# A graph layer and a mixture of experts on one Trainium2 core: events tested at every slot, another cut of the groups, row additions moved from GpSimd to VectorE

## The chip, the cores and the metric

The kernel runs on one core of one Trainium2 chip, in one launch. The metric is the device time of a run in microseconds (us), lower is better. Slots, tiles and groups are counted in the order in which the kernel works, which is from the last node to the first.

## The reference

With x of 12,500 nodes x 256 in float32, and 200,000 edges (source, destination, weight) sorted by destination:

```python
support = layernorm(x) @ W
x = x + segment_sum(support[src] * weight[:, None], dst) + b
z = layernorm(x)                      # no scale, no shift
h = gelu(einsum('nd,edf->enf', z, W1) + b1)      # 8 experts, 256 -> 512
y = einsum('enf,efd->end', h, W2) + b2           # 512 -> 256
out = x + layernorm(w_dense-weighted sum of y + z) * gamma + beta
```

The two experts and their weights are chosen once, from the mean of z over all nodes, so they are the same for every node, and are known only when the last node's z is. The destinations are dense for low node numbers (a square law), and thin for high ones.

## The kernel before

The 12,500 nodes are 98 tiles of 128. They are taken in reverse: tile 0 holds the last nodes and gets about 8 slots of edges, the last tile 158. A slot is 128 edges; there are 1563 and a remainder.

**The edge loop** (85 to 1977 us). GpSimd (POOL) gathers the 128 source rows of a slot by an indirect DMA (L588) into a ring G of 64 slots and 8 more; it waits by `s_main` (the count of finished slots) with s - RING + 3. VectorE (DVE) makes the slot's one-hot matrix OH, weighted (L1087), in a ring of eight. TensorE (PE) adds OH times G to the tile's sums (`edge`, L1451; a float32 matmul is two records, so 3126 in all). PE's program runs 8 slots per turn of a hardware loop (`slots`). Behind every odd slot it calls `event`: a While over a register test (L1460), is the next event due here. A turn ends with the loop's own code (L1486, L1491). The events are planned by `events()` and come from a table EVT:

- END, at a tile's end, 97 times: `chores` (from L1396: the transposes of the last tile's sums, their product with W, the transpose of a finished row block) and then `begin` (L1411 to L1414). As the test is at odd slots alone, a tile's end falls within a pair of slots, and `begin` retakes both of the pair with one-hot matrices OHX of the next tile, which ScalarE (ACT) made in `match` (L656, L658) and `copy` (L668). EXTRA, 7 times, is `chores` alone.
- UPS, BOTH, DOWNS, 65 in all, for 64 units. A unit is one expert's work on one group of tiles ahead of the choice: `unit_up` (L1423, z times W1) and `unit_down` (L1434, h times W2). The first 8 groups are done ahead with all 8 experts; when the experts are known, VectorE picks the two. Group 0 has two tiles, so its 8 units are half units; `by_size` (L1437 to L1442) branches on that.

`events()` spreads the units over the tiles by `room`, an estimate of what time a tile's slots leave to PE, counted from tile 14 on.

ScalarE works in sections, one per tile's end: the copy of OHX and of the tile's sums AS (L670), AT (L675), the normalized block XH (L722, needs `root`'s NR and R), then X1, the transposed block YT, a square sum, the next tile's `match`; and at the end of a section in which a group's last tile came, `root` (L702 to L716, with a table load at L704), the deviations of the group's tiles.

**The choice** of experts lies from 1977 to about 1988 us.

**The groups behind it** (1988 to 2384 us): 17 groups of four tiles (68 tiles, `post`) go through the two chosen experts, with float32 values split in a high and a low part. Per group PE runs 8 steps (L1555 to L1565 up, L1586 down). ScalarE makes Ht and Hhi (L908, L911), VectorE Hlo (L1220) and the rest: `bias` on XN (L1226), `total` (L1245 to L1259: sum, mean and variance), `give` (L1266, L1271: scale by gamma, then times the deviation plus XL). VectorE's work for a group follows two loops behind, and that for the 8 groups done ahead is put beside it, one in every second loop. POOL's `add_rows` adds the bias to XN for the groups done ahead (L605, eight times) and beta to XL for all 25 (L607); POOL's `rstd` makes the power -0.5 (L612). The last two groups go by `finish` (L1287 to L1310) in the four pieces of PARTS, with a deviation from ScalarE and VectorE. SP stores the output (L551) and loads XL (L495).

PE's side of a tile's end, as the change finds it:

```python
for r in range(n):
    if r % 4 == 0:
        e.wait_ge(s_oh, a + (r + 4))
    edge(g, r)
    if r % 2 == 1:
        event(a, r, g)
```

Of the kernel before, what the change touches and what calls it, by code (L numbers as in the profile page):

```python
# [4 lines left out]
P = 128  # L5
# [16 lines left out]
GT = 4  # L22
XG = (NT + GT - 1) // GT
SMALL = 2
NG = (NT - SMALL + GT - 1) // GT + 1
AHEAD = 8
UNITS = AHEAD * E
# [15 lines left out]
def group(t):  # L43
    return 0 if t < SMALL else (t - SMALL) // GT + 1


def tiles(g):
    a = SMALL + (g - 1) * GT
    return range(a, min(a + GT, NT)) if g else range(SMALL)


def part(t):
    return slice((t - SMALL) % GT, (t - SMALL) % GT + 1)


def place_in(t):
    return t - tiles(group(t))[0]
# [11 lines left out]
def sections():  # L69
# [14 lines left out]
def events():  # L84
# [3 lines left out]
    room = [max(0.0, 0.75 * slots[t] - 3.5) * most[t] if t >= 14 else 0.0 for t in range(NT)]  # L88
    size = [len(tiles(k // E)) / GT for k in range(UNITS)] + [1.0]
    free, u, out = 0.0, 0, []  # L90
    for t in range(NT):
        free += room[t] * sum(size) / sum(room)
        n = 0
        while u + n <= UNITS and (free >= size[u + n] / 2 or t == NT - 1):
            free -= size[u + n]
            n += 1
# [17 lines left out]
def gnn_ffn(nc, x, dflat, srct, dstt, wt, W, b, Wr, br, W1, b1t, W2, b2, gamma, beta, cst, iota_e, evt, out):  # L114
# [13 lines left out]
    with ctx:  # L128
# [26 lines left out]
        XND = sb("XND", [P, 2])  # L155
# [34 lines left out]
        OHX, OHT = early("OHX", [P, 2, P]), early("OHT", [P, 2, 2, P])  # L190
# [106 lines left out]
        s_xn, s_xb, s_xc, s_xp = sem("act_xn"), sem("pool_xn"), sem("dve_xn"), sem("pool_x1")  # L297
# [83 lines left out]
        def _(e):  # L381
# [79 lines left out]
            for t, _, kind, n in EVENTS:  # L461
# [11 lines left out]
                if kind in (END, EXTRA):  # L473
                    keep_rows(n)
                    if n == tiles(post[0])[0] + 4 * GT:
                        for t in tiles(post[0]):
                            e.wait_ge(yt_st[t % 4], 16 * (t // 4 + 1))
                        e.dma_start(YL0[:, :, :], yt_d[post[0], :, :, :]).then_inc(yl_in[0], 16)
# [12 lines left out]
            e.dma_start(YL[:, 1, :, :], yt_d[post[1], :, :, :]).then_inc(yl_in[1], 16)  # L491
# [42 lines left out]
            for n, g in enumerate(order):  # L534
# [11 lines left out]
                elif n == NG - 1:  # L546
                    for _, some in PARTS[1:]:
# [13 lines left out]
        def _(e):  # L561
# [37 lines left out]
            def add_rows(n):  # L599
                g = order[n]  # L600
                m = len(tiles(g))
                e.wait_ge(s_xn, n + 1)
                if g < AHEAD:
                    e.wait_ge(s_b2, 2)
                    e.tensor_tensor(out=XN[:, n % 3, 0:m, :], in0=XN[:, n % 3, 0:m, :], in1=B2[:, :].unsqueeze(1).to_broadcast([P, m, D]), op=ALU.add).then_inc(s_xb, 1)  # L605
                e.wait_ge(gb_in, 32)
                e.tensor_tensor(out=XL[:, n % 4, 0:m, :], in0=XL[:, n % 4, 0:m, :], in1=be_bc[:, :].unsqueeze(1).to_broadcast([P, m, D]), op=ALU.add).then_inc(s_xp, 1)  # L607

# [5 lines left out]
            added = 0  # L614
            for n in range(NG):
                until = min(n + (2 if n + 1 < NG and order[n + 1] < AHEAD else 1), NG - 1)
                while added <= until:
                    add_rows(added)
                    added += 1
                if n < NG - 2:  # L620
                    rstd(n)

        @block.scalar
        def _(e):
# [25 lines left out]
            def match(t):  # L650
                e.load([row_r], THR[0:1, t - 1:t])
                odd = e.snap(row_r, min_val=1, max_val=NE - 1)
                step(e.activation(XND[:, :], ND[:, bass.ds(odd - 1, 2)], ACT.Identity, bias=t128_row[:, t:t + 1]))
                e.wait_ge(s_act, chain)
                for k in range(2):
                    step(e.activation(OHT[:, 0, k, :], iota, ACT.Abs, bias=XND[:, k:k + 1]))  # L656
# [1000 lines left out]
```

## Time and profile before

| | us |
|---|---|
| median of 3 runs | 2390.43 |
| lowest, highest | 2388.29, 2390.5 |
| span of the profiled execution | 2384.3 |
| PE busy in the span | 2211.0 (93%) |
| PE weight loads | 1730.4 (73%) |
| VectorE | 1052.3 (44%) |
| ScalarE | 1193.0 (50%) |
| POOL | 1598.6 (67%) |

The span is counted from the first instruction to the last of one profiled execution; no whole-run time stands beside it, and the runs' median is 6.1 us longer. Engine names in the rows: PE is TensorE's matmuls, PEld its weight loads, PEldq the instructions of its sequencer (registers, branches, semaphores), DVE VectorE, ACT ScalarE, POOL GpSimd, SPq the DMA issues of SyncE. In a row by source the three durations are the least, the median and the largest in ns, and behind them stand the first and the last start in us. "[4.13 <-X]" is the engine's idle time before the row and what ended it; "issue" is a wait that the profile puts down to nothing but the instruction not having been issued. The edge loop takes four fifths of the span. Matmul records overlap: their distance is shorter than their duration.

### The profile page before, as it was taken

How to read it: one execution, taken by the hardware profiler on the slowest of the kernel's cores; microseconds unless marked ns; L12 is line 12 of the kernel's file. 1: busy time of each engine (PE TensorE's matmuls, PEld its weight loads, DVE VectorE, ACT ScalarE, POOL GpSimd, SP SyncE). 2: the span in 40 equal slices, each digit the busy share in tenths (PEclk: the TensorE clock that was granted, in tenths of full speed). 3: DMA queues.
4: the chain of work that ended last, by engine and by line, in shares of the span. 5: the costliest groups of instructions: out<-in, count | busy, mean ns of one | idle time of the engine just before them, and what ended most of it. 6: DMA issues, size and time to landing. Idle time of an engine off the chain costs nothing. (4 is left out here: it accounts for less than half of the span.)

```text
span 2384.3 us, 41652 instructions
## 1 busy us (share of the span) xinstructions
PE 2211.0 (93%) x9949; PEld 1730.4 (73%) x9950; DVE 1052.3 (44%) x2924; ACT 1193.0 (50%) x3203; POOL 1598.6 (67%) x1626
## 2 busy tenths in 40 slices
PE   2488999899999999999999999999998999999998
PEld 1366777676776777777777777777776777999997
DVE  7883223232232223232322323232222235899999
ACT  3577667665665555545534343322324116656654
POOL 6777777777777777777777777777777772242341
PEclk9999999999999999999999999999999999999999
DMA  9955667665656665566656655656565554333422
GB/s 371 333 170 156 203 203 241 186 188 180 184 183 182 179 176 175 178 185 192 186 176 189 189 172 188 182 169 190 179 193 165 183 162 135 101 113 110 134 92 68
DMA packets 226740, 425.79 MB, mean 179 GB/s; under 512 B 36675, under 2 KB 134774, under 8 KB 226600
## 3 DMA queue, kind: packets, MB, share of 16 engines
q0 software_dynamic: 75008, 204.90, 28.6%
q1 hardware_dynamic: 151160, 217.12, 27.9%
q10 hardware_dynamic: 432, 2.40, 0.3%
q14 instruction: 113, 0.93, 0.1%
q8 instruction: 27, 0.44, 0.1%
HBM read 341.53 MB, written 82.75 MB: 178 GB/s over the span
## 5 line engine op out<-in xcount | busy, mean ns | idle before, releaser
L588 POOL DMA_INDIRECT G<-xr_d,SRC x1467 | 1391.7, 949 | 446.9 <-issue 302.5
L1087 DVE TENSOR_SCALAR OH<-CST,DL,WR 128x128 f32<-128x128 f32 x1563 | 569.2, 373 | 1271.0 <-PE ps L1451 1140.1
L1451 PE MATMUL ps<-G,OH 128*128 x3126 | 739.5, 389 | 78.7 <-DVE OH L1087 58.7
L1451 PEld LDWEIGHTS ps<-G,OH 128*128 128x128 f32 x3126 | 596.7, 194 | 224.8 <-issue 143.3
L1434 PE MATMUL ps<-W2u,H 128*128 128x256 f32 x1920 | 430.6, 382 | 6.8 <-issue 6.0
L1423 PE MATMUL ps<-YU,W1u 128*128 128x512 f32 (+1 forms) x1024 | 426.4, 569 | 9.7 <-ACT H L783 8.5
L1434 PEld LDWEIGHTS ps<-W2u,H 128*128 128x128 f32 x1920 | 362.7, 191 | 69.4 <-issue 20.8
L1423 PEld LDWEIGHTS ps<-YU,W1u 128*128 128x128 f32 x1024 | 195.1, 191 | 206.3 <-issue 184.9
L791 ACT ACTIVATE YE<-ps 128x512 f32<-128x512 f32 (+1 forms) x128 | 72.6, 569 | 442.2 <-PE ps L1434 442.1
L783 ACT ACTIVATE H<-ps,b1a 128x512 f32<-128x512 f32 (+1 forms) x256 | 168.6, 661 | 226.1 <-PE ps L1423 225.8
L612 POOL TENSOR_TENSOR ZR<-ZV,mhalf 128x4 f32<-128x4 f32 (+1 forms) x23 | 31.4, 1366 | 218.0 <-DVE ZV L1259 218.0
L668 ACT ACTIVATE OHX<-OHT,WR 128x128 f32<-128x128 f32 x194 | 67.4, 394 | 211.9 <-PE ps L1451 209.0
L908 ACT ACTIVATE Ht<-ps,b1s 128x512 f32<-128x512 f32 x136 | 93.8, 690 | 129.5 <-PE ps L1565 93.6
L1586 PE MATMUL ps<-W2h,Hlo 128*128 128x256 f32 x512 | 144.9, 283 | 0.0
L1586 PE MATMUL ps<-W2l,Hhi 128*128 128x256 f32 x512 | 144.8, 283 | 0.0
L1586 PE MATMUL ps<-W2h,Hhi 128*128 128x256 f32 x512 | 144.2, 282 | 0.0
L588 POOL DMA_INDIRECT G<-in_x,SRC x96 | 92.7, 965 | 42.7 <-issue 25.9
L1220 DVE TENSOR_TENSOR Hlo<-Ht,Hhi 128x512 fp32r<-128x512 f32 x136 | 108.2, 810 | 20.3 <-ACT Hhi L911 20.3
L1402 PE MATMUL ps<-Wsb,AT 128*128 128x256 f32 x416 | 108.0, 382 | 0.7 <-ACT ps L690 0.7
L1586 PEld LDWEIGHTS ps<-W2h,Hhi 128*128 128x128 f32 x512 | 97.8, 191 | 5.6
L1586 PEld LDWEIGHTS ps<-W2l,Hhi 128*128 128x128 f32 x512 | 97.8, 191 | 5.0
L1586 PEld LDWEIGHTS ps<-W2h,Hlo 128*128 128x128 f32 x512 | 97.8, 191 | 0.0
(221 smaller groups left out, 2395.8 us busy)
## 6 DMA issues: line engine op xcount, KB each, us to landing
W1u<-in_W SPq DMA_DIRECT2D x64, 512.0 KB
W2u<-in_W SPq DMA_DIRECT2D x64, 512.0 KB
y_d<-YE SPq DMA_DIRECT2D x56, 512.0 KB, 5.4
G<-xr_d,SRC POOLq DMA_INDIRECT x1467
x_d<-X SPq DMA_DIRECT2D x98, 128.0 KB
yt_d<-YT SPq DMA_DIRECT2D x98, 128.0 KB, 3.3
XR<-in_x SPq DMA_DIRECT2D x97, 128.0 KB, 3.2
XL<-x_d SPq DMA_DIRECT2D x24, 512.0 KB, 4.7
```

What stands on the lines that cost most here:

```text
L588: e.indirect_dma_start(out=G[0:rows(s), held(s), :], out_offset=None, in_=x if s < FRESH else xr_d, in_offset=bass.IndirectOffsetOnAxis(ap ...
L668: e.activation(OHX[:, k, :], OHT[:, 1, k, :], ACT.Copy, scale=WR[:, bass.ds(odd + k, 1)]).then_inc(s_ohx, 1)
L783: e.activation(H[:, i, 0:w], ps[:, UP[i % 2], 0:w], ACT.Gelu, bias=b1a[:, u % E, i:i + 1]).then_inc(s_gelu, 1)
L791: e.activation(YE[:, u % 2, p * w:(p + 1) * w], ps[:, DN[p], 0:w], ACT.Copy).then_inc(s_ye, 1)
L908: e.activation(Ht[:, i % HB, 0:w], ps[:, 4 + i % HB, 0:w], ACT.Gelu, bias=b1s[:, i // 4, i % 4:i % 4 + 1]).then_inc(s_ht, 1)
L1087: e.tensor_scalar(OH[:, s % OHR, :], iota, DL[:, s:s + 1], WR[:, s + 1:s + 2], ALU.is_equal, ALU.mult).then_inc(s_oh, 1)
L1220: e.tensor_tensor(out=Hlo[:, h, 0:w], in0=Ht[:, i % HB, 0:w], in1=Hhi[:, h, 0:w].bitcast(f32), op=ALU.subtract).then_inc(s_hlo, 1)
L1402: e.matmul(ps[:, XB, 0:D], AT[:, c * P:(c + 1) * P], Wsb[:, c, :], start=False, stop=True, skip_group_check=True)
L1423: ins = e.matmul(ps[:, UP[i % 2], 0:m * P], W1u[:, c, i * P:(i + 1) * P], YU[:, c, 0:m * P], start=(c == 0), stop=(c == 1))
L1434: ins = e.matmul(ps[:, DN[p], h * D:(h + 1) * D], H[:, i, j * P:(j + 1) * P], W2u[:, i, :], start=(h == 0 and i == 0), stop=(i == 3), skip ...
L1451: e.matmul(ps[:, 0, 0:D], OH[:, r, :], Gf[:, bass.ds(g + r * D, D)], start=False, stop=True, skip_group_check=True).then_inc(s_main, 1)
L1586: ins = e.matmul(acc, hp[:, h, rows], wp[:, x_, f, :], start=(i == 0 and q % 2 == 0 and a == 0), stop=(i == HID - 1 and a == 2), skip_grou ...
```

## The change

- The event test stands behind every slot, and the tables give a tile's end to the slot; `begin` retakes one slot, OHX and OHT are half as large, `match` and `copy` make one matrix. POOL's wait is s - RING + 2.
- `root` is called one section later, behind AT and ahead of the normalized block.
- The groups are cut anew: nine of four, one of two, fifteen of four. So the 8 groups done ahead are all full (32 tiles in place of 30), `by_size` goes, 17 groups with 66 tiles are left for behind the choice, and the second of these is that of two tiles. `room` is 0.8 x slots - 3.0, from tile 15 on.
- POOL's `add_rows` goes. VectorE does it in `stored_bias` and `beta_rows`, placed in steps of its loops. POOL keeps `rstd`, now for the last group but one too, which goes by `total` and `give`; PARTS has three pieces, all of the last group.

```diff
-SMALL = 2
-NG = (NT - SMALL + GT - 1) // GT + 1
 AHEAD = 8
+SMALL = NT - AHEAD * GT - (NT - AHEAD * GT) // GT * GT
+SIZES = [GT] * (AHEAD + 1) + [SMALL] + [GT] * ((NT - AHEAD * GT) // GT - 1)
+STARTS = [sum(SIZES[:g]) for g in range(len(SIZES))]
+NG = len(SIZES)
...
-        root = together.get(x1)
+        root = together.get(copied[v - 3]) if v >= 3 else None
+        waiting += root or []
         xh = waiting.pop(0) if waiting else None
-        waiting += root or []
...
-    room = [max(0.0, 0.75 * slots[t] - 3.5) * most[t] if t >= 14 else 0.0 for t in range(NT)]
-    size = [len(tiles(k // E)) / GT for k in range(UNITS)] + [1.0]
+    room = [max(0.0, 0.8 * slots[t] - 3.0) * most[t] if t >= 15 else 0.0 for t in range(NT)]
     free, u, out = 0.0, 0, []
     for t in range(NT):
-        free += room[t] * sum(size) / sum(room)
+        free += room[t] * (UNITS + 1) / sum(room)
...
-        PARTS = ((NG - 2, slice(0, len(tiles(order[NG - 2])))), (NG - 1, slice(0, 2)), (NG - 1, slice(2, 3)), (NG - 1, slice(3, 4)))
+        PARTS = (slice(0, 2), slice(2, 3), slice(3, 4))
...
-                    e.wait_ge(s_main, s - RING + 3)
+                    e.wait_ge(s_main, s - RING + 2)
...
-            def add_rows(n):
...
-            added = 0
-            for n in range(NG):
-                until = min(n + (2 if n + 1 < NG and order[n + 1] < AHEAD else 1), NG - 1)
-                while added <= until:
-                    add_rows(added)
-                    added += 1
-                if n < NG - 2:
-                    rstd(n)
+            for n in range(NG - 1):
+                rstd(n)
...
-                for k in range(2):
-                    e.activation(OHX[:, k, :], OHT[:, 1, k, :], ACT.Copy, scale=WR[:, bass.ds(odd + k, 1)]).then_inc(s_ohx, 1)
+                e.activation(OHX[:, :], OHT[:, 1, :], ACT.Copy, scale=WR[:, bass.ds(cut + 1, 1)]).then_inc(s_ohx, 1)
...
+                if s["root"] is not None:
+                    root(s["root"])
                 if s["xh"] is not None:
                     normal(v, s["xh"])
...
-                if s["root"] is not None:
-                    root(s["root"])
...
+            def stored_bias(n):
+                m = len(tiles(order[n]))
+                e.wait_ge(s_xn, n + 1)
+                e.wait_ge(s_b2, 2)
+                e.tensor_tensor(out=XN[:, n % 3, 0:m, :], in0=XN[:, n % 3, 0:m, :], in1=B2[:, :].unsqueeze(1).to_broadcast([P, m, D]), op=ALU.add).then_inc(s_xb, 1)
+
+            def beta_rows(n):
+                m = len(tiles(order[n]))
+                e.wait_ge(gb_in, 32)
+                e.wait_ge(s_xn, n + 1)
+                e.tensor_tensor(out=XL[:, n % 4, 0:m, :], in0=XL[:, n % 4, 0:m, :], in1=be_bc[:, :].unsqueeze(1).to_broadcast([P, m, D]), op=ALU.add).then_inc(s_xp, 1)
...
+                    if k >= 2 and k % 2 == 0 and i == 2:
+                        beta_rows(n)
                     if two and i == 2:
+                        stored_bias(n + 1)
                         total(n + 1, None, slice(0, 2))
...
+                    if two and i == 6:
+                        beta_rows(n + 1)
+                    if k >= 2 and k % 2 == 0 and i == 7 and k < len(post) - 1:
+                        beta_rows(place[post[k - 1]])
...
+                    if i == 5 and k == len(post) - 1:
+                        beta_rows(NG - 2)
                     if i == 6 and k == len(post) - 1:
                         bias(k)
+                        beta_rows(NG - 1)
+            n = NG - 2
+            total(n, len(post) - 2, slice(0, 2))
+            total(n, len(post) - 2, slice(2, 4))
+            give(n, slice(0, 4))
             for j in range(len(PARTS)):
                 finish(j)
...
             def begin(v, g):
-                e.wait_ge(s_ohx, v * 2)
+                e.wait_ge(s_ohx, v)
                 e.wait_ge(s_as, v + 1)
-                e.matmul(ps[:, 0, 0:D], OHX[:, 0, :], Gf[:, bass.ds(g, D)], start=True, stop=False, skip_group_check=True)
-                e.matmul(ps[:, 0, 0:D], OHX[:, 1, :], Gf[:, bass.ds(g + D, D)], start=False, stop=True, skip_group_check=True).then_inc(s_begin, 1)
+                e.matmul(ps[:, 0, 0:D], OHX[:, :], Gf[:, bass.ds(g, D)], start=True, stop=True, skip_group_check=True).then_inc(s_begin, 1)
...
-            def by_size(do):
...
                         with e.If(now > UPS):
-                            by_size(unit_down)
+                            unit_down(e.snap(u_r, min_val=0, max_val=UNITS - 1))
...
                         with e.If(now == END):
-                            begin(e.snap(v_r, min_val=1, max_val=FINAL), g + (r - 1) * D)
+                            begin(e.snap(v_r, min_val=1, max_val=FINAL), g + r * D)
...
                     edge(g, r)
-                    if r % 2 == 1:
-                        event(a, r, g)
+                    event(a, r, g)
...
-        "iota_e": (np.arange(NE) // 2 * 2).astype(np.float32)[None], "evt": evt,
+        "iota_e": np.arange(NE, dtype=np.float32)[None], "evt": evt,
```

## Rows read from the trace of the kernel before

**Rows 1.** Windows: busy us (instructions) by engine, clock, DMA share, GB/s.
```profile
700.00:1100.00 400.00, 383.84 (x1575) 287.88 (x1574) 117.57 (x323) 211.09 (x624) 302.63 (x320) 0.99 0.60 180
...
2001.00:2362.00 361.00, 361.00 (x2305) 328.10 (x2306) 338.68 (x620) 224.65 (x390) 113.08 (x56) 1.00 0.31 105
```

**Rows 2.** By source, gathers (L588) and edge matmuls (L1451): ns, starts.
```profile
L588 POOL DMA_INDIRECT G<-xr_d,SRC x1467: 903/946/1013, 136.1 to 1973.5; - x184
...
L1451 PE MATMUL ps<-G,OH x3126: 379/379/791, 85.2 to 1976.8; 128*128 x195, 128*128 128x256 f32 x1
```

**Rows 3.** Waits: us in total, times, longest.
```profile
DVE OH L1087 <- PE ps L1451: 1140.1, 230, 19.3
...
PEld ps L1451 <- issue: 143.3, 216, 47.3
...
DVE OH L1087 <- DMA G<-xr_d,SRC: 44.9, 37, 14.0
...
PE ps L1413 <- ACT AS L670: 35.7, 12, 4.1
...
PE ps L1423 <- ACT H L783: 8.5, 5, 3.6
```

**Rows 4.** By source, 1656.1 to 1659.7 (last: 1656.75 to 1657.15), eight slots.
```profile
L1451 PE MATMUL ps<-G,OH x16: 379/379/478, 1656.3 to 1659.6; 128*128 x16
...
L1451 PEldq FUSED_REGOPS  x9: 46/46/51, 1656.2 to 1659.7; - x9
...
L1460 PEldq MOVE  x4: 37/37/37, 1656.5 to 1658.4; - x4
...
L1460 PEldq COMPARE_BRANCH  x4: 201/204/207, 1656.6 to 1658.5; - x4
...
L1451 PEldq FUSED_REGOPS  x2: 46/46/46, 1656.8 to 1657.0; - x2
```

**Rows 5.** By source, the tests (L1460), whole span.
```profile
L1460 PEldq MOVE  x950: 37/37/38, 85.4 to 1975.5; - x190
```

**Rows 6.** By source, L1451, 1206 to 1208.5, behind a unit.
```profile
L1451 PEldq FUSED_REGOPS  x6: 46/46/51, 1206.3 to 1207.8; - x6
...
L1451 PE MATMUL ps<-G,OH x2: 379/379/379, 1208.2 to 1208.4; 128*128 x2
```

**Rows 7.** By source, L1460 then L1396, 1651 to 1653, a tile's end.
```profile
L1460 PEldq MOVE  x1: 37/37/37, 1651.5 to 1651.5; - x1
...
L1396 PEldq EVENT_SEMAPHORE  x1: 51/51/51, 1652.3 to 1652.3; - x1
```

**Rows 8.** Timeline of PE: start, us, count; a full unit, then half units.
```profile
1194.33 7.17 PE L1434 MATMUL ps<-W2u,H 128*128 128x256 f32 x32 [0.31 <-issue]
...
1201.33 7.03 PE L1423 MATMUL ps<-YU,W1u 128*128 128x512 f32 x16
...
232.61 3.62 PE L1434 MATMUL ps<-W2u,H 128*128 128x256 f32 x16
...
240.41 1.77 PE L1451 MATMUL ps<-G,OH 128*128 x7
```

**Rows 9.** Timeline of PE from 227 us.
```profile
227.59 1.22 PE L1413 MATMUL ps<-G,OHX 128*128 x2 [4.13 <-ACT AS L670]
...
229.45 3.32 PE L1451 MATMUL ps<-G,OH 128*128 x8
```

**Rows 10.** By source, DVE L1266 and L1226.
```profile
L1266 DVE SCALAR_TENSOR_TENSOR Z<-Z,ZMV,g_bc x90: 468/476/2639, 2037.2 to 2360.9; 128x256 f32<-128x256 f32 x90
...
L1226 DVE TENSOR_TENSOR XN<-XN,B x17: 1206/1210/1218, 2019.2 to 2364.4; 128x1024 f32<-128x1024 f32 x17
```

**Rows 11.** Timeline of ACT, 2050 to 2056.
```profile
2050.63 2.08 ACT L842 ACTIVATE XN<-XL,NR,R 128x256 f32<-128x256 f32 x4 [7.29 <-DMA XL<-x_d]
```

**Rows 12.** Timeline of DVE, 2355 to 2384.
```profile
2362.09 0.68 DVE L1220 TENSOR_TENSOR Hlo<-Ht,Hhi 128x512 fp32r<-128x512 f32 x1
...
2365.56 0.68 DVE L1220 TENSOR_TENSOR Hlo<-Ht,Hhi 128x512 fp32r<-128x512 f32 x1
```

More of the change, by code:

```diff
@@ L43, in group, with place_in @@
 def group(t):
-    return 0 if t < SMALL else (t - SMALL) // GT + 1
+    return max(g for g in range(NG) if STARTS[g] <= t)
 def tiles(g):
-    a = SMALL + (g - 1) * GT
-    return range(a, min(a + GT, NT)) if g else range(SMALL)
+    return range(STARTS[g], STARTS[g] + SIZES[g])
+def place_in(t):
+    return t - STARTS[group(t)]
 def part(t):
-    return slice((t - SMALL) % GT, (t - SMALL) % GT + 1)
-def place_in(t):
-    return t - tiles(group(t))[0]
+    return slice(place_in(t), place_in(t) + 1)
 def slot(t):
@@ L490, in _ @@
                 e.wait_ge(yt_st[t % 4], 16 * (t // 4 + 1))
-            e.dma_start(YL[:, 1, :, :], yt_d[post[1], :, :, :]).then_inc(yl_in[1], 16)
+            w = len(tiles(post[1])) * P
+            e.dma_start(YL[:, 1, :, 0:w], yt_d[post[1], :, :, 0:w]).then_inc(yl_in[1], 16)
             def load_x1(n):
@@ L546, in _ @@
                 elif n == NG - 1:
-                    for _, some in PARTS[1:]:
+                    for some in PARTS:
                         e.wait_ge(s_fin, first_of[n] + some.stop)
@@ L651, in match @@
                 e.load([row_r], THR[0:1, t - 1:t])
-                odd = e.snap(row_r, min_val=1, max_val=NE - 1)
-                step(e.activation(XND[:, :], ND[:, bass.ds(odd - 1, 2)], ACT.Identity, bias=t128_row[:, t:t + 1]))
+                cut = e.snap(row_r, min_val=0, max_val=NE - 1)
+                step(e.activation(XND[:, :], ND[:, bass.ds(cut, 1)], ACT.Identity, bias=t128_row[:, t:t + 1]))
                 e.wait_ge(s_act, chain)
-                for k in range(2):
-                    step(e.activation(OHT[:, 0, k, :], iota, ACT.Abs, bias=XND[:, k:k + 1]))
+                step(e.activation(OHT[:, 0, :], iota, ACT.Abs, bias=XND[:, 0:1]))
                 e.wait_ge(s_act, chain)
-                step(e.activation(OHT[:, 1, :, :], OHT[:, 0, :, :], ACT.Relu, bias=ones[:, 0:1], scale=-1.0))
+                step(e.activation(OHT[:, 1, :], OHT[:, 0, :], ACT.Relu, bias=ones[:, 0:1], scale=-1.0))
             def copy(v, t):
                 e.load([thr_r], THR[0:1, t:t + 1])
-                odd = e.snap(thr_r, min_val=1, max_val=NE - 1)
-                e.wait_ge(s_main, odd + 1)
+                cut = e.snap(thr_r, min_val=0, max_val=NE - 1)
+                e.wait_ge(s_main, cut + 1)
                 if t:
@@ L929, in _ @@
             e.activation(r1[:, 6:7], eps[:, 0:1], ACT.Abs_reciprocal_sqrt)
-            for j, (n, some) in enumerate(PARTS):
-                e.wait_ge(s_zv, NG - 2 + j + 1)
+            n = NG - 1
+            for j, some in enumerate(PARTS):
+                e.wait_ge(s_zv, n + j + 1)
                 e.activation(ZR[:, n % 3, some], ZV[:, n % 3, some], ACT.Abs_reciprocal_sqrt).then_inc(s_seed, 1)
@@ L1278, in finish @@
             def finish(j):
-                n, some = PARTS[j]
-                k, qs = len(post) - 2 + (n == NG - 1), range(some.start, some.stop)
+                n, k, some = NG - 1, len(post) - 1, PARTS[j]
+                qs = range(some.start, some.stop)
                 for q in qs:
@@ L1422, in unit_up, with unit_down @@
                     for c in range(2):
-                        ins = e.matmul(ps[:, UP[i % 2], 0:m * P], W1u[:, c, i * P:(i + 1) * P], YU[:, c, 0:m * P], start=(c == 0), stop=(c == 1))
+                        ins = e.matmul(ps[:, UP[i % 2], :], W1u[:, c, i * P:(i + 1) * P], YU[:, c, :], start=(c == 0), stop=(c == 1))
                     ins.then_inc(s_up, 1)
-            def unit_down(u, m):
+            def unit_down(u):
                 e.wait_ge(w2_in, u * 16 + 16)
@@ L1430, in unit_down @@
                     e.wait_ge(s_ye, u * 2 + (p + 1))
-                    for h in range(m // 2):
-                        j = m - 1 - (m // 2 * p + h)
+                    for h in range(GT // 2):
+                        j = GT - 1 - (GT // 2 * p + h)
                         for i in range(4):
@@ L1468, in event @@
                         with e.If(now < DOWNS):
-                            by_size(unit_up)
+                            unit_up(e.snap(u_r, min_val=0, max_val=UNITS - 1))
                     with e.Else():
@@ L1512, in _ @@
                 edge(g, r)
-                if r % 2 == 1:
-                    event(a, r, g)
+                event(a, r, g)
             e.sem_inc(s_main, 1)
```

42 lines of the change are left out of this document (15 added, 27 removed).

## The prediction

> **What bounds the kernel now.** I read the windows by stretch first. In the edge loop (85 to 1977 us) and behind it PE is nearly always busy: 383.84 of 400 us from 700 to 1100, and all of the 361 us from 2001 to 2362 [rows 1]. The edge loop's pace, however, is POOL's: the rows by source show 1467 gathers from 136.1 to 1973.5, so 1.25 us each, of which 0.95 is the gather, and the last edge matmul starts at 1976.8, 3 us behind the last gather [rows 2]. The waits say how near PE is to that pace [rows 3]. VectorE waited 44.9 us for gathered rows (that is PE's real slack, about 47 us with what passes on to PE), and PE's weight loads waited 143.3 us for "issue", which is PE's own sequencer; 47.3 of it is one wait at the start, so 96 us are spread over 215 waits. PE has thus under 150 us to spare in 1867, and two thirds of that is already lost to its sequencer. The reader should see two bounds lying on each other.
>
> The rows of one undisturbed stretch of 8 slots tell the sequencer's cost [rows 4]. Its nine dispatch records go from 1656.2 to 1659.7: 3.45 us for 8 slots. The 16 matmuls, 0.216 us apart, take the same 3.46. Two slots and one test are 0.63 us (three intervals between four MOVEs, 1656.5 to 1658.4); a test's two records alone are 0.037 + 0.207 = 0.244, and two dispatches can't be more than the rest, 0.39. From the test's MOVE at 1656.5 the next dispatch starts at 1656.8, the one behind it at 1657.0. I take 0.36 for a test and 0.13 to 0.14 for a dispatch (2 × 0.135 + 0.36 = 0.63; bounds for the test: 0.244, its records, and 0.4, the widest that the printed tenths allow). So 8 × 0.135 + 4 × 0.36 = 2.5, and the loop's end makes the other 0.95.
>
> **Part 1: a test behind every slot.** Now there are 950 tests [rows 5], 781 at odd slots (1562/2) and 169 repeated, one behind each event. The change adds one at each even slot: 781 × 0.36 = **+281 us** of sequencer time, 1.44 per 8 slots (4.89 instead of 3.45, against 3.46 of matmuls). Behind the test stand the next slot's two matmuls; behind these, s_main: VectorE's one-hot ring and POOL's gather ring wait for it. VectorE has time (it waits 1140 us for PE). POOL can be about 60 gathers ahead, and once that is used up it waits for PE. What takes from the 281:
> - Behind a unit the sequencer is ahead: six dispatches from 1206.3 on, the first matmul at 1208.2, so 1.9 us of queued work [rows 6]. Each of 64 units pays for that much of the lag: 64 × 1.9 = **−122**. Behind a tile's end the lead is only some 0.1.
> - It costs at an event's start. From the test at 1651.5 to the first instruction of the chores at 1652.3 are about 0.9 us, and a dispatch of 0.13 [rows 7]. Now a queue of matmuls covers that; with an empty one only the last slot's, about 0.5, so some 0.55 us of PE idle at each of 161 events: **+88**.
> - by_size goes: one branch less ahead of each half of a unit, which I have left in the lead and cost at nothing.
>
> **Part 2: one slot retaken.** One matmul pair of 0.43 less at 97 ends, of which 0.2 goes back because the sequencer has less cover there: 97 × 0.23 = **−22**. ScalarE loses an OHX copy and an Abs, both beside PE's work. POOL may start a gather one slot later behind PE than before, since one slot less is retaken, so its wait loosens by a slot; at a ring of 64 I count nothing.
>
> **Part 3: sizes.** Eight half units become full. A full one lasts 1194.33 to 1208.2 = 13.87 us, a half one 232.61 to 240.41 = 7.80, 0.54 of that waiting for H [rows 8]. The five waits for H, 8.5 us in all [rows 3], take about 4 more off: 8 × 6.07 − 4 = **+45** in the edge loop. The shifted due times (15 tiles before the first, 0.8 and 3.0) I cost at nothing: the load is spread in proportion to room either way; what they could do is part of the range.
>
> **Part 4: root a section later.** ScalarE's chain behind a group's last tile holds PE's retake: 12 waits of PE, 35.7 us [rows 3], one of 4.13 us at 227.59 [rows 9]. Between two copies of AS ScalarE has the same work as before, less 0.7 us, so the stall moves on by one section. Bounds: 0 and −36. Since PE comes later to every tile's end in part 1, ScalarE gains time whatever the order; I take **−20**.
>
> **PE's slack.** The 47 us in which PE had run out of gathered slots are filled first: **−47**.
>
> Edge loop: 281 − 122 + 88 − 22 + 45 − 20 − 47 = **+203**; it would end near 2180 in place of 1977.
>
> **Part 5: behind the edge loop.** From 2001 to 2362 PE runs 16 groups of four tiles without a gap, 361 us or 22.56 each [rows 1]. Two tiles less: 22.56/4 × 2 = **−11.3**. VectorE was busy 338.68 of the 361, so it decides whether PE keeps this. POOL adds beta once in each of 25 groups and the stored bias in eight; beside such an add a VectorE operation of 0.476 us lasts up to 2.639 [rows 10]. Taking 33 of them away gives back up to 33 × 2.16 = 71 us; doing them on VectorE costs 33 × 1.21 = 40 (by L1226, same shape). VectorE falls by some 31, and stays under PE. The group of two is second, however, so PE comes out of the loops around it 11.3 us sooner. There a chain stands that does not shrink with it: VectorE's end of the first group, the store, the XL load behind it on SP's queue, for which ScalarE waited 7.29 us until 2050.63 [rows 11], and ScalarE's next H. Two new adds on VectorE, 2 × 1.21, come in front of it. PE did not stall there before; putting that margin at 0.6 (an estimate), I take **+1.8** (bounds 0 and 7.3, the whole of that wait).
> The tail is VectorE's. Two bias adds and two L1220 run from 2362.1 to the last L1220 at 2365.56 [rows 12], late by these four, for ScalarE has no more H to give behind 2362. With VectorE no longer late this is **−3.5** (bounds: 0, and −5 if the last group but one, which leaves the finishing chain for the ordinary one with POOL's rstd, gains there too). Together **−13**. The start-up is unchanged.
>
> **Sum.** The profiled execution spans 2384.3; the median of the runs is 2390.43, 6.1 more, which I carry over. 2390.4 + 203 − 13 = 2580.4, so **2580 us**.
>
> **Rivals.**
> - *The tests are covered (faster).* PE's queue could hold enough work that the tests run behind matmuls and the loop stays POOL's. It decides if the lead behind units and ends averaged over 1.8 us per event, or a test cost under 0.2. For it: the six dispatches ahead [rows 6], and that matmuls (3.46) and sequencer (3.45) tie now [rows 4]. Against: nothing hides 4.89 behind 3.46, and 96 us of issue waits are there already. The loop then ends where POOL ends, and only the −13 stay: 2377. Chance 0.13 (0.01 of it within 0.2%).
> - *A test costs its records alone.* 0.037 + 0.207 = 0.244 us, not 0.36: 781 × 0.12 = 94 less, 2487. For: the dispatch gap of 0.13 may overlap it. Against: [rows 4]. Chance 0.09.
> - *The clock falls.* PE now idles between slots. Behind a stall of 4.13 us the next 8 matmuls, four slots, took 3.32 us, 0.83 a slot in place of 0.43 [rows 9], the lower of two clock levels (1.2 and 2.4 GHz); otherwise the granted clock is 0.97 to 1.00 in this loop. If a sixth of the slots ran like that, 0.83 − 0.61 = 0.22 more each, and their units' matmuls doubled too: +60, 2640. Chance 0.05. The Trainium skill, "TensorE: Matmul & The Clock Gate", section on a second HAM failure mode, says that short idles between groups of matmuls can make the clock go back and forth; by that rule the whole loop would be exposed. At 0.22 on all 1563 slots the time would be 2580 + 344 = 2924; I give that 0.01 of the 0.05. Against it stand the 96 us of short issue waits in a loop with its clock at 0.97 and more.
> - *VectorE becomes the bound behind the loop.* If the operations stay long without POOL's adds (another cause), VectorE has 338.7 + 40 = 379 us of work against PE's 350: +29, 2609. Chance 0.03.
> - *The root's move does what it says* and all 36 us of stalls go: 2564, inside the first case.
>
> **How the numbers follow.** First case 0.70, with its own range 2520 to 2640: the lead of 1.9 could be used up less (±40), the 0.55 could be 0.2 or 0.8 (±50), the root 0 or −36. The range of 8 in 10 leaves out the covered case and thin tails: 2450 to 2650. A measurement of this kernel tells about 0.2% from no change. Faster by more 0.12, within 0.01, slower 0.87.
>
> **What would show it.** Right: about 1730 tests at L1460 in place of 950; 8 plain slots take 4.9 us, not 3.45; waits of PE's weight loads at L1451 for issue rise from 143 to over 250 us; POOL's waits for PE get long, not only many; the last edge matmul near 2180; no POOL adds, no L1266 over 0.6 us; the tail 3 us shorter. Wrong: gathers still 1.25 us apart to the end (covered), 8 slots in 4.0 us (records alone), a granted clock under 0.95 over long stretches, PE waiting for VectorE behind the loop.

## The result, and the profile after

The changed kernel takes 2553.16 us (median of 4 runs, 2552.18 to 2555.29) against 2389.36 (4 runs) before: ratio 1.0693, interval 1.068 to 1.0705, slower by 164 us. The forecast was 2580, with 2520 to 2640 as the likeliest case's own range.

The page of the changed kernel, its span and part 1:

```profile
span 2551.1 us, 42441 instructions
...
PE 2315.9 (91%) x9835; PEld 1622.8 (64%) x9836; DVE 1024.0 (40%) x2953; ACT 1138.3 (45%) x3006; POOL 1521.6 (60%) x1594
```

By source: the tests (now L1464), the edge matmuls (L1455) and the gathers (L590), with their first and last starts:

```profile
L1464 PEldq MOVE  x1732: 29/37/38, 85.5 to 2152.4; - x193
...
L1455 PE MATMUL ps<-G,OH x3126: 379/379/790, 85.5 to 2152.7; 128*128 x195, 128*128 128x256 f32 x1
...
L590 POOL DMA_INDIRECT G<-xr_d,SRC x1467: 902/947/1017, 141.0 to 2114.9; - x184
```

The tests have gone from 950 [rows 5] to 1732. The last edge matmul starts at 2152.7 in place of 1976.8 [rows 2], so the edge loop holds +176 us; what lies behind it is 2551.1 - 2152.7 = 398.4 in place of 2384.3 - 1976.8 = 407.5, so -9. POOL's last gather is issued at 2114.9, 38 us ahead of the last matmul; before, 3 us [rows 2]. The pace is PE's.

By source, eight slots without an event (2132.2 to 2137.1), the answer to [rows 4]:

```profile
L1455 PE MATMUL ps<-G,OH x16: 379/405/478, 2132.4 to 2136.2; 128*128 x16
...
L1455 PEldq FUSED_REGOPS  x8: 46/46/51, 2132.3 to 2135.8; - x8
...
L1464 PEldq MOVE  x8: 29/37/37, 2132.4 to 2135.9; - x8
```

Eight tests stand where there were four. Such a turn takes 4.83 to 4.95 us from its first dispatch to that of the next turn in the 28 without an event behind 1000 us (median 4.88); the prediction's sum was 4.89. Without a test the next dispatch comes 0.13 us later, with one 0.49: 0.36 for a test.

The waits that answer to [rows 3] (total, times, longest):

```profile
DVE OH L1072 <- PE ps L1455: 1278.4, 446, 16.9
...
PEld ps L1455 <- issue: 423.0, 1127, 47.3
...
POOL G L590 <- PE ps L1455: 287.1, 487, 11.1
...
PE ps L1455 <- DVE OH L1072: 115.9, 109, 46.5
...
PE ps L1425 <- ACT AS L654: 12.2, 8, 2.0
```

Two rows more of that kind, first of the kernel before, then PE's timeline of the changed one at the start of the turn above:

```profile
POOL G L588 <- PE ps L1451: 141.3, 454, 3.3
```

```profile
2132.37 4.21 PE L1455 MATMUL ps<-G,OH 128*128 x16 [0.63 <-DVE OH L1072]
```

Issue waits of the weight loads rose from 143.3 to 423.0 us and from 216 to 1127 times: at seven slots in ten PE has nothing queued. POOL waits for PE 287.1 us in place of 141.3 (the longest 11.1 and not 3.3), and VectorE 1278.4 in place of 1140.1. PE's waits for OH are the sequencer's too: but for the first two (46.5 us at the start of the loop, 3.7 at 97.6) they are 107 waits of 0.3 to 0.7 us, 66 us in all, and stand where a turn begins. The first load of a turn carries the wait for OH, but VectorE was itself waiting for PE there; what ended last was the loop's own code. ScalarE's AS holds PE for 12.2 us and no longer 35.7.

Behind the edge loop, PE's timeline at the loop's end and at the only longer gap of the groups, then ScalarE's row beside it (start, length, idle time before and its end), and by source the branch of the last test:

```profile
2151.43 1.68 PE L1455 MATMUL ps<-G,OH 128*128 128x256 f32 x6 [0.31 <-issue]
...
2156.06 0.69 PE L1499 MATMUL ps<-CST,AS 128*128 128x128 f32 x2 [2.95 <-ACT AS L837]
...
2225.02 0.70 PE L1557 MATMUL ps<-YTh,W1h 128*128 128x512 f32 x2 [1.62 <-issue]
```

```profile
2221.69 2.08 ACT L826 ACTIVATE XN<-XL,NR,R 128x256 f32<-128x256 f32 x4 [8.19 <-DMA XL<-x_d]
```

```profile
L1464 PEldq COMPARE_BRANCH  x1: 2984/2984/2984, 2152.5 to 2152.5; - x1
```

PE stood still 2.95 us for AS, where the kernel before had 0.47. AS itself waited for PE's sequencer, whose last test of the loop, at 2152.5, took 2.984 us to branch, where the median is 0.201. The first matmul of the groups comes 14.9 us behind the last edge matmul and not 10.9. The gap of 1.62 us at 2225.02 is the one that the prediction put at 1.8: ScalarE had waited 8.19 us for XL, and then had its next H late. VectorE's operations that POOL's adds had stretched [rows 10], by source:

```profile
L1263 DVE SCALAR_TENSOR_TENSOR Z<-Z,ZMV,g_bc x94: 468/476/485, 2212.8 to 2537.8; 128x256 f32<-128x256 f32 x94
...
L1211 DVE TENSOR_TENSOR XN<-XN,B x17: 684/1215/1217, 2194.1 to 2530.4; 128x1024 f32<-128x1024 f32 x16, 128x512 f32<-128x512 f32 x1
```

The longest L1263 takes 0.485 us; before, 2.639.

### The profile page after: what moved, and what is told of

Its sections match the earlier page's. It is cut to its first block and busy times, and to the rows that moved or that the text cites. A ratio compares the mean times of both kernels' runs of the same rounds, so it can differ in the third digit from the quotient of the medians.

```text
span 2551.1 us, 42441 instructions
## 1 busy us (share of the span) xinstructions
PE 2315.9 (91%) x9835; PEld 1622.8 (64%) x9836; DVE 1024.0 (40%) x2953; ACT 1138.3 (45%) x3006; POOL 1521.6 (60%) x1594
## 5 line engine op out<-in xcount | busy, mean ns | idle before, releaser
L590 POOL DMA_INDIRECT G<-xr_d,SRC x1467 | 1396.7, 952 | 578.4 <-issue 300.0
L1072 DVE TENSOR_SCALAR OH<-CST,DL,WR 128x128 f32<-128x128 f32 x1563 | 567.0, 366 | 1443.9 <-PE ps L1455 1278.4
L1455 PE MATMUL ps<-G,OH 128*128 x3126 | 814.1, 407 | 142.1 <-DVE OH L1072 115.9
L1455 PEld LDWEIGHTS ps<-G,OH 128*128 128x128 f32 x3126 | 518.1, 191 | 452.7 <-issue 423.0
L1445 PE MATMUL ps<-W2u,H 128*128 128x256 f32 x2048 | 458.7, 382 | 18.2 <-issue 18.1
L1434 PE MATMUL ps<-YU,W1u 128*128 128x512 f32 x1024 | 450.3, 592 | 1.9 <-issue 1.5
L1445 PEld LDWEIGHTS ps<-W2u,H 128*128 128x128 f32 x2048 | 383.9, 190 | 92.6 <-issue 42.9
L775 ACT ACTIVATE YE<-ps 128x512 f32<-128x512 f32 x128 | 76.3, 596 | 519.5 <-PE ps L1445 519.5
L767 ACT ACTIVATE H<-ps,b1a 128x512 f32<-128x512 f32 x256 | 175.8, 687 | 240.3 <-PE ps L1434 240.1
L652 ACT ACTIVATE OHX<-OHT,WR 128x128 f32<-128x128 f32 x97 | 39.0, 402 | 292.4 <-PE ps L1455 289.6
L892 ACT ACTIVATE Ht<-ps,b1s 128x512 f32<-128x512 f32 (+1 forms) x136 | 92.1, 677 | 121.9 <-PE ps L1567 119.8
L590 POOL DMA_INDIRECT G<-in_x,SRC x96 | 92.8, 967 | 47.4 <-issue 26.2
L1205 DVE TENSOR_TENSOR Hlo<-Ht,Hhi 128x512 fp32r<-128x512 f32 (+1 forms) x136 | 90.4, 669 | 34.3 <-ACT Hhi L895 34.1
```

The costliest lines, as they stand in the source:

```text
L590: e.indirect_dma_start(out=G[0:rows(s), held(s), :], out_offset=None, in_=x if s < FRESH else xr_d, in_offset=bass.IndirectOffsetOnAxis(ap ...
L652: e.activation(OHX[:, :], OHT[:, 1, :], ACT.Copy, scale=WR[:, bass.ds(cut + 1, 1)]).then_inc(s_ohx, 1)
L767: e.activation(H[:, i, 0:w], ps[:, UP[i % 2], 0:w], ACT.Gelu, bias=b1a[:, u % E, i:i + 1]).then_inc(s_gelu, 1)
L775: e.activation(YE[:, u % 2, p * w:(p + 1) * w], ps[:, DN[p], 0:w], ACT.Copy).then_inc(s_ye, 1)
L892: e.activation(Ht[:, i % HB, 0:w], ps[:, 4 + i % HB, 0:w], ACT.Gelu, bias=b1s[:, i // 4, i % 4:i % 4 + 1]).then_inc(s_ht, 1)
L1072: e.tensor_scalar(OH[:, s % OHR, :], iota, DL[:, s:s + 1], WR[:, s + 1:s + 2], ALU.is_equal, ALU.mult).then_inc(s_oh, 1)
```

## The experiments

Nine kernels ran, three of them twice, in three lots. The first four runs were on a chip on which the kernel before takes 3233 us and not 2390, with a granted clock of 0.86 to 0.88 in the edge loop of before_bare_tests; why it is slow stays open. Three of the four were tried again on another chip (2388 for before). Ratios are those within a lot; places in the traces are compared across the chips on which before takes 2388 to 2389 us.

**A test behind every slot, whole body.** The kernel before, with nothing due at even slots:

```diff
-                with e.While(lambda: e.snap(rel) <= r):
+                with e.While(lambda: e.snap(rel) <= r - (r % 2 == 0)):
...
-                            begin(e.snap(v_r, min_val=1, max_val=FINAL), g + (r - 1) * D)
+                            begin(e.snap(v_r, min_val=1, max_val=FINAL), g + (max(r, 1) - 1) * D)
...
-                    if r % 2 == 1:
-                        event(a, r, g)
+                    event(a, r, g)
```

> The kernel before, with the event test of the change (its whole body with it) behind the even slots too, where no event is ever due; nothing else changes, and no work is left out. Sequencer theory: 781 more tests of 0.36 us less what the leads cover; 2389 + about 175 = 2565 (2530 to 2600), the last edge matmul near 2150. Rival, the other parts of the change (sizes, retaking, root) carry the loss: at most 2420.

Measured: 7505.57 us, ratio 2.3194 (2.3092 to 2.3296). Neither theory has this. Its page, part 3, and by source the branches of the tests, with one row of PE's timeline:

```profile
q8 instruction: 1970, 32.28, 1.9%
```

```profile
L1460 PEldq COMPARE_BRANCH  x1730: 69/2916/6582, 133.9 to 7088.9; - x193
...
3002.48 1.21 PE L1451 MATMUL ps<-G,OH 128*128 x2 [2.01 <-issue]
```

The instruction queue moved 32.28 MB in 1970 packets in place of 0.44 MB in 27: ten packets for each of 195 turns. The median branch of a test takes 2.916 us, and PE mostly waits 2.0 to 2.3 us ahead of a slot. So the loop of eight bodies, each with a half and a full unit, is loaded anew in every turn.

**Exact ends alone.** The kernel before with the change's test, tables, `match`, `copy` and `begin`, and `by_size` kept:

```diff
-                            begin(e.snap(v_r, min_val=1, max_val=FINAL), g + (r - 1) * D)
+                            begin(e.snap(v_r, min_val=1, max_val=FINAL), g + r * D)
...
-                    if r % 2 == 1:
-                        event(a, r, g)
+                    event(a, r, g)
```

> The kernel before with exact ends: a test behind each slot (whole bodies, both unit sizes), one slot retaken; sizes, root and adds as before. If only the test counts: 2389 + 147 as with bare tests, less some 20 for the retaken slot, 2515 to 2540. Rival, the loop with eight bodies of both unit sizes doesn't fit and is loaded again each turn, as with before_all_tests (1970 packets on the instruction queue): far over 3000.

Measured: 7438.6 us, ratio 3.1145 (3.1098 to 3.1193), 1972 packets on the instruction queue. The named rival is what happened. PE's timeline, the instruction queue and the granted clock (page, parts 3 and 2) of this kernel, and under them the changed kernel's queue and clock:

```profile
3013.93 1.22 PE L1448 MATMUL ps<-G,OH 128*128 x2 [2.11 <-issue]
...
3017.23 1.21 PE L1448 MATMUL ps<-G,OH 128*128 x2 [2.08 <-issue]
```

```profile
q8 instruction: 1972, 32.31, 2.0%
...
PEclk8556665565656566566656666666656556665599
```

```profile
q8 instruction: 28, 0.46, 0.1%
...
PEclk9999999999999999999999999999999999999999
```

With some 2 us of idle behind nearly every slot, and 8 where a turn begins, the granted clock is 0.60 in the mean from 2000 to 7000 us. The changed kernel, with the same eight tests, has 28 packets and its clock: PE's loop differs from this one's in `by_size` alone, which puts the code of a half unit beside that of a full one in each body. So two parts of the change that look apart hang together: without the new cut, which makes all units full, the tests at every slot cost not 150 us but 5000. What exact ends and the one retaken slot cost by themselves this run therefore can't tell.

**A bare test behind even slots.** No body to jump over:

```diff
                     if r % 2 == 1:
                         event(a, r, g)
+                    else:
+                        with e.While(lambda: e.snap(rel) <= r - 64):
+                            e.reg_mov(now_r, e.snap(kind))
```

> The kernel before, with a test of the same register behind the even slots whose body is one register move and is never entered. Sequencer theory: the test itself costs, so as with the whole body, 2565 within 20. Rival, the longer program (four more event bodies a turn to jump over) costs through instruction loading: clearly less, under 2480.

On the slow chip it took 3275.19 us, ratio 1.012 (1.0059 to 1.018); what covers the tests there was not looked into. Again where before takes 2388:

> The same kernel as before_bare_tests (before, and behind each even slot a test that is never true, with a body of one register move). After the run with whole bodies, in which the instruction queue moved 1970 packets in place of 27, the test and the loading of instructions are two costs. Where before takes 2390: sequencer theory 2565 within 30, the last edge matmul near 2150, 27 packets on the instruction queue. Rival, a test costs nothing unless instructions must be loaded: under 2420.

Measured: 2536.76 us, ratio 1.0616 (1.0593 to 1.064). By source and by waits:

```profile
L1486 PEldq MOVE  x780: 29/37/38, 85.6 to 2123.9; - x195
...
L1451 PE MATMUL ps<-G,OH x3126: 379/379/791, 85.6 to 2126.5; 128*128 x195, 128*128 128x256 f32 x1
```

```profile
PEld ps L1451 <- issue: 379.4, 1056, 47.5
...
POOL G L588 <- PE ps L1451: 260.1, 475, 11.1
...
PE ps L1413 <- ACT AS L670: 15.4, 11, 2.5
```

780 tests more move the last edge matmul from 1976.8 to 2126.5, and the instruction queue keeps its 27 packets. 150 us, for the change's 176 in the edge loop, come with the bare test alone: a test costs sequencer time, whatever stands behind it. The time is 28 us under the middle of what was expected, at the edge of its range. And PE's waits for AS fall from 35.7 to 15.4 us, though `root` is where it was.

**The change without tests at every slot.** Sizes, root and VectorE's adds as changed; tests and retaking as before (its diff is the change's own, without those parts):

```diff
-                            begin(e.snap(v_r, min_val=1, max_val=FINAL), g + r * D)
+                            begin(e.snap(v_r, min_val=1, max_val=FINAL), g + (r - 1) * D)
...
-                    event(a, r, g)
+                    if r % 2 == 1:
+                        event(a, r, g)
```

> The changed kernel with the tests at odd slots alone and both slots of the pair retaken, as before; sizes, root and VectorE's adds as changed. Sequencer theory: the edge loop is POOL's again, its last matmul at 1977 to 2000 (the eight fuller units eat PE's slack), 9 us less behind it, so 2380 to 2405. Rival, fuller units and moved due times carry part of the loss: 2420 or more.

Slow chip: 3228.07 us, ratio 0.9983 (0.9961 to 1.0005). On the other:

> The same kernel as pairs_kept (the change with tests at odd slots and both slots of a pair retaken), wanted on a chip on which the kernel before takes 2390 and not 3233 us. There, sequencer theory: the edge loop ends at 1977 to 2000 and the run takes 2380 to 2405. Rival, fuller units and moved due times carry part of the loss: 2420 or more.

Measured: 2386.28 us, ratio 0.9993 (0.9983 to 1.0002), no difference from before. So all that the changed kernel loses comes with the test at every slot, the exact ends and the one retaken slot.

```profile
L1458 PE MATMUL ps<-G,OH x3126: 379/379/790, 84.8 to 1989.2; 128*128 x195, 128*128 128x256 f32 x1
```

```profile
POOL G L590 <- PE ps L1458: 141.1, 463, 0.3
...
PE ps L1427 <- ACT AS L656: 20.8, 9, 2.5
```

The loop ends at 1989.2, and 393.8 us lie behind it, 13.7 less than before: the prediction's -13 without the 4 us lost at the loop's end.

**A test ahead of each pair.** The changed kernel, with single tests only where the pair has an event:

```diff
+                    if r % 2 == 0:
+                        with e.If(e.snap(rel) > r + 1):
+                            for q in range(r, r + 2):
+                                edge(g, q)
+                        with e.Else():
+                            for q in range(r, r + 2):
+                                edge(g, q)
+                                event(a, q, g)
```

> The changed kernel with one test ahead of each pair of slots: if no event is due in the pair, two slots without tests, else each with its own test as changed. Exact ends and one slot retaken stay. Sequencer theory: about 1290 tests in place of 1731, the extra ones only near events; some 440 x 0.36 = 158 us of sequencer time less, so 2395 to 2440, the lower if the leads reach. Rival, exact ends or the single retaken slot cost by themselves: over 2480.

Slow chip: 3257.21 us, ratio 1.006 (1.0034 to 1.0085). On the other:

> The same kernel as after_guard2 (the change, with one test ahead of each pair and single tests only in pairs with an event). Where before takes 2390: sequencer theory 2395 to 2440. Rival, exact ends or the single retaken slot cost by themselves: over 2480.

Measured: 2463.85 us, ratio 1.0317 (1.0297 to 1.0336): outside the expected 2395 to 2440, and short of the rival's 2480.

```profile
L1464 PEldq MOVE  x504: 29/29/34, 97.4 to 2056.3; - x168
...
L1455 PE MATMUL ps<-G,OH x3126: 379/379/791, 84.9 to 2056.6; 128*128 x195, 128*128 128x256 f32 x1
```

504 tests and 780 guards (the test ahead of a pair) end the loop at 2056.6, 96 us earlier than 1732 tests. But an If with an Else costs more than a While's test, for the common way jumps over the other at its end, with a branch of 0.169 us of its own: an empty turn takes 3.73 to 4.13 us (median 3.81), where with the tests at odd slots the median is 3.46. The distances between the starts of PE's matmuls settle the rival. Against pairs_kept they are 65 us longer between slots and 29 at the starts of events, but 27 shorter at `begin` and behind it: the one retaken slot gives time and costs none.

**VectorE's adds alone.** The kernel before with `stored_bias`, `beta_rows` and the shorter PARTS:

```diff
-            def add_rows(n):
...
+            for n in range(NG - 1):
+                rstd(n)
...
+                    if k >= 2 and k % 2 == 0 and i == 2:
+                        beta_rows(n)
```

> The kernel before with POOL's row additions done by VectorE as in the change, the last group but one by total and give; tests, retaking, root and groups as before. Theory: VectorE's long operations beside POOL go, the adds cost less than they; PE still bounds the groups, the tail is 3.5 us shorter: 2386 where before takes 2390. Rival, VectorE becomes the bound behind the edge loop: 2400 or more.

Measured: 2384.5 us, ratio 0.9983 (0.9973 to 0.9993).

```profile
L1463 PE MATMUL ps<-G,OH x3126: 378/379/791, 85.6 to 1977.3; 128*128 x195, 128*128 128x256 f32 x1
```

The loop is unchanged, the stretch behind it is 2380.9 - 1977.3 = 403.6, so -4, nearly all of it behind PE's last matmul. It is the only kernel here whose interval lies under 1, by 0.17% in the median, and so the fastest.

**The new cut alone, and the later root alone.**

```diff
-SMALL = 2
-NG = (NT - SMALL + GT - 1) // GT + 1
+SIZES = [GT] * (AHEAD + 1) + [SMALL] + [GT] * ((NT - AHEAD * GT) // GT - 1)
```

> The kernel before with the new cut of the groups and the new due times alone (by_size gone). Theory: the eight fuller units push the edge loop's end from 1977 to about 1990, two tiles less give back 11 behind it: 2388 to 2393, no difference. Rival, the later root is what moved the end to 1989 in pairs_kept: 2378 to 2382.

Measured: 2399.96 us, ratio 1.006 (1.0045 to 1.0076), slower.

```profile
L1446 PE MATMUL ps<-G,OH x3126: 379/379/791, 84.8 to 1999.0; 128*128 x195, 128*128 128x256 f32 x1
```

22 us later at the loop's end, 10.9 less behind it.

```diff
-        root = together.get(x1)
+        root = together.get(copied[v - 3]) if v >= 3 else None
```

> The kernel before with root called one section later alone. Theory: PE's waits for ScalarE's AS only move on by a section, and POOL sets the loop's pace anyway: within 3 us of before, its last edge matmul within 3 us of 1977. Rival: the waits go (36 us in the profile of before) and the loop ends 5 us or more earlier.

Measured: 2387.16 us, ratio 0.9998 (0.9989 to 1.0008), the last edge matmul where it was:

```profile
L1451 PE MATMUL ps<-G,OH x3126: 379/379/792, 84.7 to 1977.1; 128*128 x195, 128*128 128x256 f32 x1
```

```profile
PE ps L1413 <- ACT AS L670: 16.5, 8, 2.4
...
PE ps L1402 <- ACT ps L690: 12.4, 6, 5.8
...
DVE OH L1087 <- DMA G<-xr_d,SRC: 161.0, 141, 14.5
```

The waits for AS fell from 35.7 to 16.5 us, but most of that has moved: ahead of the product with W PE now waits 12.4 us for ScalarE (L690), where it waited 0.7 before. Some 7 us of 36 are gone. Where POOL sets the pace that is worth nothing (VectorE now waits 161.0 us for gathered rows in place of 44.9). With the cut alone the loop ends at 1999.0, with cut and root (and adds, which run later) at 1989.2: about 10 where PE's own work is longer.

**One test for four empty slots**, tried as the version to beat both:

```diff
                     if r % 4 == 0:
+                        with e.If(e.snap(rel) <= r + 3):
+                            for q in range(r, r + 4):
...
+                                edge(g, q)
+                                if q % 2 == 1:
+                                    event(a, q, g)
+                        with e.Else():
...
+                                edge(g, q)
```

> pairs_kept, with one more test ahead of each four slots: where no event is due in them they run without tests, the branch laid so that this common way has no jump at its end. Sizes, root and VectorE's adds as in the change. Sequencer theory: the two tests of an empty four become one, which gives PE's sequencer about 0.36 us in each of some 220 fours and costs it 0.4 to 0.6 in each of some 165 others, where units' leads cover part; the edge loop's end moves from 1989 towards POOL's own 1977, 2372 to 2388 in all, under the kernel before. Rival, the extra test near events is what counts (as after_guard2 showed, 2464 where 2395 to 2440 was expected): over 2392.

Measured: 2399.09 us, ratio 1.0048 (1.0035 to 1.0062). The rival was right.

```profile
L1458 PE MATMUL ps<-G,OH x3126: 379/379/791, 85.0 to 2006.6; 128*128 x195, 128*128 128x256 f32 x1
...
L1467 PEldq MOVE  x502: 37/37/38, 86.6 to 2003.9; - x168
```

There are 502 tests and 390 guards, 892 in place of 950, and the sequencer's empty turns have a median of 3.2 us in place of 3.46; yet the loop ends at 2006.6, 17 us later than in pairs_kept. The distances of PE's starts say where: from the last matmul of `begin` to the next slot's, 90 times, it is 51.4 us in all and not 36.0. All of these 15 us stand at the 51 tile ends in the last pair of a four, where the jump over the other branch and the next guard come before the next slot. Behind a tile's end PE has little queued.

## Why the prediction was right, point by point

The sign, the size and the mechanism held: the sequencer bounds the edge loop at 4.89 us a turn, POOL waits for PE, the tail gets shorter. That the sum came within 27 us is in part luck, for its two largest errors, +23 and -49, have opposite signs. The terms, taken from the distances of PE's starts in the two traces, summed by what follows what (140 us to the last edge matmul):

| step of the prediction | forecast | measured |
|---|---|---|
| between slots (tests +281, leads -122, slack -47) | +112 | +135 (660.4 to 795.6) |
| the start of an event, 0.55 each | +88 | +39 (43.2 to 82.4) |
| one slot retaken | -22 | -29 (102.2 to 73.0, `begin` and what follows it) |
| eight half units made full | +45 | +43 (804.5 to 847.3) |
| root and AS | -20 | -23 (47.7 to 24.8) |
| not foreseen: from the transposes to the product with W, which now waits for ScalarE | 0 | +6 (11.6 to 18.0) |
| everything else | 0 | +4 |
| edge loop | +203 | +176 |
| two tiles less | -11.3 | -10.9 (the cut alone) |
| the XL chain | +1.8 | +1.6 |
| the tail | -3.5 | -3.7 |
| not foreseen: from the loop to the groups | 0 | +4.1 |
| behind the loop | -13 | -9 |

From 2580 to 2553 it is 27 less in the loop, 4 more behind it, and 4 less because the median of the runs lies 2.1 us above the span in the changed kernel, where the prediction carried over 6.1.

**A test's cost**, read from two slots and one test, was right: 0.36.

**Between the slots** the tests, the leads behind units and the slack were forecast as one sum, +112. The bare tests gave +109, so as a sum it held. That the slack in it was 47 is not shown: it was read from VectorE's waits for gathered rows, and these did not go (53.6 us with bare tests, 62.1 in the changed kernel). What stood between slots before, beyond their 0.216 us of distance, was 41 us in all (660.4 for 2866 distances). The 1867 us given there for the length of the loop are 1892 by [rows 2]; nothing rests on them. The changed kernel's +135 is 26 more than the bare tests', nearly all of it between slots that follow a tile's end (+109 against +87 us; behind units +27 against +22). There one slot less is retaken, which leaves the sequencer less cover (argued, not tried alone). The prediction had 19 of that in its -22; both rows together were +90 and are +106.

**The term that was mis-sized** is the event's start, 0.55 us each in the forecast and 0.24 as measured (39 us on 160). Two things were wrong. First, the 0.9 us from the test to the first instruction of the chores are 0.8 in [rows 7], and the 0.55 is too long even for an empty queue: where the queue is empty, the first matmul of a tile's end starts 0.55 to 0.59 us behind the last slot's, so PE loses 0.33 to 0.37, and at a third of the ends the queue still covers it. Second, `by_size`, whose going the prediction cost at nothing. PE's timeline at the start of a unit with bare tests, where it is still there, and in the changed kernel:

```profile
1218.64 0.69 PE L1434 MATMUL ps<-W2u,H 128*128 128x256 f32 x2 [0.64 <-issue]
```

```profile
1237.33 0.91 PE L1445 MATMUL ps<-W2u,H 128*128 128x256 f32 x3 [0.27 <-issue]
```

With bare tests the starts of events cost 60 us, 23 at tile ends and 37 at units; in the changed kernel 39, 21 at ends and 18 at units. The difference is a register move and a branch of 0.21 us (L1440) less ahead of each unit: with a test at every slot that branch is on PE's path, and its going gave back 19 us.

**Root.** The -20 was right, and for the reason given: PE comes later to every tile's end. The bare tests show it with `root` unmoved (waits for AS 15.4 us, the distance from the chores to `begin` 47.7 to 27.1). In the changed kernel, with `root` moved as well, that distance is 24.8, and 6 us are lost ahead of the product with W. That is the part of the stall that moves on, as root_alone shows it; the prediction said that it would, but had nothing for it in its sum.

**The +45** of the fuller units was right in the changed kernel (+43). With tests at odd slots the cut costs 22: the units take 38 more, the slots between them 10 less and the starts of units 7 less.

**Behind the loop** 4 us were missed. The 2.95 us ahead of L1499 are the last test's branch of 2.984 us. It is as long as the branches in exact_alone (median 2.899), where the instruction queue loaded ten packets a turn. Here that queue has none from 109 us on until 2152.7, and two in the window from 2150 to 2157:

```profile
q8 instruction: 2, 0.03, 2.2%
```

So the code behind the loop had to be loaded. In the kernel before a packet starts at 1976.7, but there nothing on PE waits for it, and with odd tests and all else as changed PE's gap is 0.47 too. The rest of the 4 us goes on the matmuls behind the gap, which run slower (granted clock 0.79 in the mean from 2152 to 2168, where it was 0.87 from 1977 to 1990).

**The rivals.** Tests covered: no, by the issue waits and by the bare tests. A test costing its records alone: no, 0.36 holds. The falling clock: not in the changed kernel, whose granted clock stays at 0.9 and more in each slice, in spite of a thousand short gaps; so the rule of the Trainium skill ("TensorE: Matmul & The Clock Gate", on the second failure mode) did not show here. In exact_alone, where the gaps are 2 us and more behind nearly each slot, the clock went back and forth between its two levels and was 0.60 in the mean. VectorE as the bound: no, it falls to 320.06 busy of 360 us from 2170 to 2530. The largest danger, that eight bodies are loaded in each turn, was in no rival; the second copy of a unit's code in each body, which the change happens to take out, decides it.

## What to carry to other kernels

In a hardware loop with small matmuls count the sequencer's time per turn beside the engine's: here a register test costs 0.36 us against a slot's 0.43 of matmuls, sequencer and matmuls were level at 3.46 us a turn before, and a change that saved work on VectorE, ScalarE and POOL lost 7% by adding tests. What is added matters by its place: behind a tile's end, where little is queued, a jump is paid for, while behind a unit some 1.9 us cover it. Once the sequencer bounds the loop, a branch that cost nothing before (`by_size`) is worth 19 us. And look at the instruction queue's packets before and after any change that unrolls a loop or adds code to its body: 27 or 28 against 1970 was the difference between some 2550 and over 7400 us.

## What the runs showed of the hardware

- PE's loop of eight event bodies was loaded again in each turn with both unit sizes in the bodies (1970 packets, 32.28 MB, ten packets a turn) and not at all with one size (28 packets, none between 109 and 2152.7 us). The median branch of a test rose from 0.201 to 2.9 us.
- Where such a loop isn't reloaded, the branch out of it can still be: the changed kernel's last test took 2.984 us.
- An If with an Else makes an empty pair dearer than a While that isn't entered: an empty turn of four guards took 3.81 us (median), of four tests 3.46, which is also the time of its matmuls.
- The granted clock was 0.99 in the mean from 200 to 2150 us of the changed kernel, with over a thousand waits of the weight loads of 0.2 to 0.3 us, and 0.60 in exact_alone from 2000 to 7000, with 2 us and more behind nearly each slot.
- PE's wait for a semaphore at the first instruction of a loop's turn can be the loop's own code: 107 waits "for OH" of 0.3 to 0.7 us stand at turn starts, while VectorE waits for PE.
- One chip ran the kernel before in 3233 us in place of 2388, and on it 780 more tests cost 1.2% in place of 6.2%. What slows it is not known.
